# ACT writes the biases of keys and values into the banks ahead of the products, for 14 of 32 pairs

## The chip, the cores and the metric

One core of a Trainium2 chip. The time is the device time of one execution, in microseconds, as the median of several runs. A profiled execution gives a trace; its instants below are counted from the span's start. The names of the engines are PE (TensorE), DVE (VectorE), ACT (ScalarE), POOL (GpSimd) and SP (the queue that issues most DMAs).

## What is computed

One layer over 8 sequences of 1024 rows of width 256: attention with linear kernel features and no softmax, a residual and two layer norms, then a gated feed-forward of width 704 on weights and activations rounded in blocks of 16 to a four-bit grid, a residual and a layer norm. What the change touches is the first part:

```python
q = split(x @ Wq + bq);  k = split(x @ Wk + bk);  v = split(x @ Wv + bv)   # 16 heads of 16
q = elu(q) + 1;  k = elu(k) + 1
k = k / sqrt(sum(k * k, over a head) + eps)
attn = (q @ k.T) @ v          # per head; done as q @ (k.T @ v)
x = layernorm(x + layernorm_affine(x + attn @ Wo + bo))
# then w = four-bit blocks of the ffn weights, h = silu(x' @ wg) * (x' @ wu), x = layernorm(x + h' @ wd)
```

## The kernel before

The 8192 rows are 64 tiles of 128, worked in 32 pairs, four pairs to a sequence. Every engine has its own queue, written out by hand as a loop over steps p, and semaphores tie the queues together. Pairs 0 to 23 run alone (`first`); from step 24 (`MERGE`) on the second stage (`step`) is woven in, and from step 36 it runs alone.

PE in `first(p)`: transposes of x of pair p+1 (line 388), the products of keys and values of pair p (`kv_project`, lines 377 to 379 and the bias product at line 401), at some steps a turn of feed-forward weights (`weights_turn`, line 452), the accumulation of k.T v of pair p-2 (line 415), the query products of pair p-1, and at every fourth step `kv_out` (line 444). Every fp32 product is three fp32r products of high and low parts. The bias of the keys, and the 1 of elu + 1, are added by a small product of `rows` (ones times a two-row split of bk + 1) into the first 256 columns of a bank. Two pairs of banks take turns (`kv_banks`).

ACT: the high part of the transposes (line 574), the seeds of pair p-1 (lines 590, 591, 593), the queries of pair p-2 (599, 602), then the exponential of pair p's keys (608), the squares (613) and a weight chunk's conversion (581).

DVE: the low part of the transposes (756), query features (790), key features (800), then `v_bias` (806) that adds bv to the values while it takes them from the bank, sums of squares (813), the scales of a chunk of weights (760 to 768) and the rounding of a chunk (776, 778).

POOL: the Newton steps of pair p-1 (1036, 1038, 1040, 1043), normalised keys (1049, raises `k_hat`), x plus biases for the later residuals (1059, twice a pair), a weight chunk's scaling (1022), and the multiply that puts a rounded chunk back (1029, raises `w_deq`).

The feed-forward weights are rounded in 11 chunks during this stage, and their transposes (turns) are put at steps 8, 9, 12, 13, 16, 18, 22, 23, 24 and 25 (`WG_STEP`). A turn waits for the last chunk that it needs:

```python
def weights_turn(g):
    pe.wait_ge(w_deq, wg_chunks(g))
    after(pe, wT_lo, g)
```

The turns at steps 8, 12, 16, 18, 22 and 24 need 2, 4, 6, 7, 9 and 11 chunks. A chunk is put back in the pass of POOL just ahead of step 8, 12, 16, 18, 22 or 24.

Of the kernel before, what the change touches and what calls it, by code (L numbers as in the profile page):

```python
# [10 lines left out]
ALU = mybir.AluOpType  # L11
# [22 lines left out]
def build(nc, x, Wq, bq, Wk, bk, Wv, bv, Wo, bo, gamma, beta, w_gate, w_up, w_down, out):  # L34
# [21 lines left out]
    with ExitStack() as ctx:  # L56
# [3 lines left out]
        def sem(name):  # L60
            return ctx.enter_context(nc.semaphore(name))
# [14 lines left out]
        gamma_b = sb("gamma_b", [P, D])  # L76
        bq_c, bq_neg, bq_one = (sb(n, [P, KT]) for n in ("bq_c", "bq_neg", "bq_one"))
# [48 lines left out]
        bv_b, bo_b = words(9587, D), words(9843, D)  # L126
# [38 lines left out]
        def f32(a):  # L165
# [9 lines left out]
        wk_in, wv_in, wq_in, wffn_in, rows_in, bv_in, bq_in, xb_in, late_in = (  # L175
            sem(n) for n in ("wk_in", "wv_in", "wq_in", "wffn_in", "rows_in", "bv_in", "bq_in", "xb_in", "late_in"))
# [9 lines left out]
        xT_ps, xT_hi_s, xT_lo_s = sem("xT_ps"), sem("xT_hi_done"), sem("xT_lo_done")  # L186
        kv_ps, k_exp, k_feat, v_s, k_sq, k_ssq, k_se, k_log, k_seed = (
# [79 lines left out]

        def mo_bank(b):
            return Q_BANK if b < B - 1 else KV_BANK + 1
# [34 lines left out]
        def _(sp):  # L304
# [11 lines left out]
            sp.dma_start(beta_b[:, :], beta.partition_broadcast(P)).then_inc(xb_in, 16)  # L316
            load_x(2)
# [54 lines left out]
        def _(pe):  # L372
            def split_product(dst, stat, mov, n, ended=True, shared=False):

                for k in range(n):
                    (sh, sl), (mh, ml) = stat(k), mov(k)
                    nc.tensor.matmul(dst, sl, mh, start=(k == 0), stop=False, skip_group_check=shared)  # L377
                    nc.tensor.matmul(dst, sh, ml, start=False, stop=False, skip_group_check=shared)  # L378
                    last = nc.tensor.matmul(dst, sh, mh, start=False, stop=(ended and k == n - 1), skip_group_check=shared)  # L379
                return last  # L380
# [11 lines left out]
            def kv_project(p):  # L392
                pe.wait_ge(xT_lo_s, p + 1)
                after(pe, k_feat, kv_read(p))
                after(pe, v_s, kv_read(p))
                for jj in range(2):
                    bank = kv_banks(p) + jj
                    c = slice((p % PPB) * 2 * P + jj * P, (p % PPB) * 2 * P + (jj + 1) * P)
                    split_product(ps[:, bank, :], lambda k: (xT_hi[:, k, c], xT_lo[:, k, c]),
                                  lambda k: (wkv_hi[:, k, :], wkv_lo[:, k, :]), KT, ended=False, shared=True)  # L400
                    last = nc.tensor.matmul(ps[:, bank, 0:D], rows[:, D:], rows[:, 0:D], start=False, stop=True,  # L401
                                            skip_group_check=True)
                last.then_inc(kv_ps, 1)
# [161 lines left out]
        def _(act):  # L565
# [43 lines left out]

            def k_squares(p):  # L610
                act.wait_ge(k_feat, p + 1)
                after(act, k_ssq, p)
                nc.scalar.activation(ksq, kf[:, p % 2, :], ACT.Square).then_inc(k_sq, 1)
# [6 lines left out]
            def first(p):  # L620
# [16 lines left out]
                if p >= 7 and (p - 7) % PPB == 0 and (p - 7) // PPB < B:  # L637
                    kv_out_copy((p - 7) // PPB)
                if pair(p - 1):
                    k_seeds(p - 1)  # L640
# [98 lines left out]
        def _(dve):  # L739
# [63 lines left out]
            def v_bias(p):  # L803
                after(dve, kv_acc, p - 2)
                b = kv_banks(p)
                nc.vector.tensor_tensor(vb[:, p % 3, :, :], ps[:, b:b + 2, D:2 * D],
                                        bv_b[:, :].unsqueeze(1).broadcast_to([P, 2, D]), ALU.add).then_inc(v_s, 1)
# [366 lines left out]
```

## Time and profile before

| what | value |
|---|---|
| median of 3 runs | 708.73 us (708.36 to 708.86) |
| profiled execution, its own time | 708.65 us |
| its span, first to last instruction | 706.9 us |
| mean granted PE clock | 0.994 |
| PE busy | 687.4 us (97%) |
| PE weight loads busy | 603.9 us (85%) |
| POOL busy | 611.9 us (87%) |
| DVE busy | 593.9 us (84%) |
| ACT busy | 485.0 us (69%) |

How to read it: a busy PE is not PE at its peak, since matmuls are pipelined and their ends are modelled; the distance from one start to the next is what a product costs. An idle time stands in brackets with its releaser, which is the semaphore event that came last by the trace. A wait for several semaphores can name the wrong one.

### The profile page before, as it was taken

The page shows a single profiled execution, that of the slowest core. Times are in us where ns is not written, and L with a number is a line of the kernel's source. Part 1 is how long each engine was busy: PE and PEld are TensorE (multiplying, and loading weights), DVE is VectorE, ACT ScalarE, POOL GpSimd, SP SyncE. Part 2 cuts the span into 40 slices and gives each one's busy share as a digit, 9 for nine tenths or more (in the row PEclk, how much of TensorE's full clock was granted, in tenths as well). Part 3 has the DMA queues.
Part 4 walks back from the last instruction along what each step waited for, and adds up shares of the span by engine and source line. Part 5 has one row for each costly group of instructions (what it writes and reads, how often), then busy time and mean ns, then how long its engine had stood idle before and what let it go on. Part 6 is the DMA issues. An engine that isn't in the chain of part 4 may idle for free.

```text
span 706.9 us, 14230 instructions
## 1 busy us (share of the span) xinstructions
PE 687.4 (97%) x4370; PEld 603.9 (85%) x4370; DVE 593.9 (84%) x1448; ACT 485.0 (69%) x943; POOL 611.9 (87%) x951
## 2 busy tenths in 40 slices
PE   7999999999988999999999999999999999999995
PEld 6887878778866799999999999999999999999995
DVE  5788888885878888898898898998998898998774
ACT  4666766766667767767767767767767767767664
POOL 2989888987998999988988988988988988989766
PEclk9999999999999999999999999999999999999999
DMA  9443343344322021111111111111111111100001
GB/s 280 170 136 134 128 135 123 113 165 152 118 91 90 30 62 45 61 46 46 56 65 46 60 46 46 53 68 46 61 46 46 52 69 46 60 17 16 16 32 45
DMA packets 22272, 55.05 MB, mean 78 GB/s; under 512 B 2547, under 2 KB 5557, under 8 KB 22197
## 3 DMA queue, kind: packets, MB, share of 16 engines
q1 hardware_dynamic: 21776, 54.01, 22.5%
q8 instruction: 35, 0.57, 0.4%
q14 instruction: 41, 0.33, 0.2%
q10 hardware_dynamic: 420, 0.13, 0.1%
HBM read 28.90 MB, written 25.17 MB: 76 GB/s over the span
## 4 chain that ended last, share of the span: by engine, by line
PE 89%; POOL 4%; issue 3%; DVE 2%; ACT 1%; DMA 1%; SPq 0%; POOLq 0%; DVEq 0%; ACTq 0%
PE banks L377 23%; PE banks L379 22%; PE banks L378 22%; PE banks L519 8%; PE banks L490 7%; PE banks L415 2%; PE banks L388 2%; PE banks L533 1%; PE banks L532 1%; PE banks L401 1%; PE banks L444 1%; DMA arena<-in_L_attn_x_dram 1%; POOL arena L1126 1%; PE banks L452 1%; POOL lnbuf L1111 0%
## 5 line engine op out<-in xcount | busy, mean ns | idle before, releaser
L377 PE MATMUL banks<-wgu_hi,actT_lo 128*128 128x512 f32 (+1 forms) x384 | 149.8, 390 | 1.6 <-DVE resid L790 1.3
L378 PE MATMUL banks<-wgu_lo,actT_hi 128*128 128x512 f32 (+1 forms) x384 | 144.0, 375 | 0.0
L379 PE MATMUL banks<-wgu_hi,actT_hi 128*128 128x512 f32 (+1 forms) x384 | 143.3, 373 | 0.0
L1126 POOL TENSOR_TENSOR arena<-arena 128x960 f32<-128x960 f16 (+2 forms) x68 | 115.1, 1693 | 0.0
L688 ACT ACTIVATE arena<-banks 128x512 f32<-128x512 f32 x64 | 38.4, 599 | 111.7 <-PE banks L379 111.5
L1102 POOL TENSOR_TENSOR arena<-arena 128x704 f32<-128x704 f32 x64 | 89.1, 1392 | 21.1 <-DVE arena L907 19.0
L377 PE MATMUL banks<-wd_hi,actT_lo 128*128 128x256 f32 x320 | 100.1, 313 | 0.0
L920 DVE TENSOR_TENSOR actT_lo<-banks,actT_hi 128x512 fp32r<-128x512 f32 (+1 forms) x132 | 85.6, 674 | 16.9 <-ACT actT_hi L674 16.2
L379 PE MATMUL banks<-wd_hi,actT_hi 128*128 128x256 f32 x320 | 90.3, 282 | 0.0
L378 PE MATMUL banks<-wd_lo,actT_hi 128*128 128x256 f32 x320 | 90.2, 282 | 0.0
L377 PEld LDWEIGHTS banks<-wgu_hi,actT_lo 128*128 128x128 f32 x384 | 72.5, 189 | 11.2 <-DVE resid L790 1.7
L379 PEld LDWEIGHTS banks<-wgu_hi,actT_hi 128*128 128x128 f32 x384 | 72.2, 188 | 10.5
L378 PEld LDWEIGHTS banks<-wgu_lo,actT_hi 128*128 128x128 f32 x384 | 72.6, 189 | 7.6
L674 ACT ACTIVATE actT_hi<-banks 128x384 fp32r<-128x384 f32 (+2 forms) x132 | 63.3, 530 | 17.4 <-PE banks L519 17.4
L519 PEld LDWEIGHTS banks<-ident,arena 128*128 128x128 f32 x512 | 59.7, 140 | 12.5 <-DVE actT_lo L920 2.3
L660 ACT ACTIVATE arena<-arena 128x960 f16<-128x960 bf16 (+2 forms) x68 | 66.3, 975 | 5.8 <-POOL arena L1105 5.4
L519 PE MATMUL banks<-ident,arena 128*128 128x128 f32 x512 | 67.0, 272 | 3.4 <-DVE lnbuf L943 1.5
L929 DVE TENSOR_TENSOR arena<-arena,banks 128x512 f32<-128x512 f32 x64 | 43.9, 686 | 30.9 <-issue 26.4
L1111 POOL TENSOR_TENSOR lnbuf<-lnbuf,gamma_b 128x256 f32<-128x256 f32 x64 | 46.9, 732 | 24.4 <-ACT lnbuf L695 24.4
L1059 POOL TENSOR_TENSOR xs<-arena 128x512 f32<-128x512 f32 x48 | 61.6, 1304 | 6.6 <-DMA arena<-in_L_attn_beta_dram 6.6
L1089 POOL TENSOR_TENSOR rstd<-ve,mhalf 128x3 f32<-128x3 f32 x78 | 67.0, 858 | 0.0
L667 ACT ACTIVATE arena<-arena 128x960 uint16<-128x960 uint16 (+2 forms) x68 | 65.2, 958 | 2.2
(126 smaller groups left out, 1932.8 us busy)
## 6 DMA issues: line engine op xcount, KB each, us to landing
xs<-x_plus_scratch SPq DMA_DIRECT2D x32, 512.0 KB, 3.3
x_plus_scratch<-xs SPq DMA_DIRECT2D x24, 512.0 KB, 2.9
arena<-in_L_attn_x_dram SPq DMA_DIRECT2D x32, 256.0 KB, 3.6
out_dram<-arena SPq DMA_DIRECT2D x32, 256.0 KB, 2.1
x_plus_scratch<-arena SPq DMA_DIRECT2D x8, 512.0 KB, 2.9
resid<-in_L_ffn_w_down_dram SPq DMA_DIRECT2D x1, 704.0 KB, 7.7
resid<-in_L_ffn_w_gate_dram SPq DMA_DIRECT2D x1, 640.0 KB, 8.1
resid<-in_L_ffn_w_up_dram SPq DMA_DIRECT2D x1, 640.0 KB, 9.5
```

Of the source, the lines that this page charges most:

```text
L377: nc.tensor.matmul(dst, sl, mh, start=(k == 0), stop=False, skip_group_check=shared)
L378: nc.tensor.matmul(dst, sh, ml, start=False, stop=False, skip_group_check=shared)
L379: last = nc.tensor.matmul(dst, sh, mh, start=False, stop=(ended and k == n - 1), skip_group_check=shared)
L519: last = nc.tensor.transpose(ps[:, T_BANK + c // 4, (c % 4) * P:(c % 4 + 1) * P], va[:, (n + 1) % 2, c * P:(c + 1) * P], ident[:, :])
L660: nc.scalar.activation(vqb[n % 2][:, a // RW:b // RW, 0:RW].bitcast(F16), lines(halves(vy[:, n % 2, a:b])), ACT.Copy, scale=F16_ONE).then_ ...
L667: nc.scalar.activation(q, q, ACT.Copy, bias=ROUND_HALF).then_inc(half_s, 1)
L674: last = nc.scalar.activation(vT_hi[:, n % 2, a:whole, :], view[:, 0:whole - a, :], ACT.Copy)
L920: last = nc.vector.tensor_tensor(vT_lo[:, n % 2, a:b, :], view, f32(vT_hi[:, n % 2, a:b, :]), ALU.subtract)
L1059: nc.gpsimd.tensor_tensor(to[:, :, kind, :], xin[:, 2 * r:2 * r + 2, :], row[:, :].unsqueeze(1).broadcast_to([P, 2, D]), ALU.add).then_inc ...
L1089: nc.gpsimd.tensor_tensor(rstd[:, s, :], ve[:, :], mhalf[:, :].broadcast_to([P, 3]), ALU.pow).then_inc(pow_s, 1)
L1102: last = nc.gpsimd.tensor_tensor(blocks(vy[:, s, D:VW]), blocks(h[:, s, :]), each(inv[:, s, D // BLK:VB]), ALU.mult)
L1126: nc.gpsimd.tensor_tensor(blocks(va[:, (n + 1) % 2, a:b]), blocks(vqc[n % 2].bitcast(F16)[:, a:b]), each(s14[:, n % 2, a // BLK:b // BLK]) ...
```

## The change

For the 14 pairs from 2 to 23 that have no turn of weights in their step (`filled(p)`), ACT writes bk + 1 and bv into the pair's two banks in one activation of 128x1024 before the products, which then accumulate onto them and begin no new group. The two bias products of such a pair go, and DVE copies the values out of the bank where it added bv before. The key bias is loaded a second time, onto all partitions, and ACT adds 1.0 to it once. The activation for pair p+1 stands in ACT's `first(p)` ahead of the seeds of pair p-1. `bo_b` moves to a tile of its own.

```diff
+        bo_b = sb("bo_b", [P, D])
-        bv_b, bo_b = words(9587, D), words(9843, D)
+        bkv = words(9587, 2 * D)
+        bv_b = bkv[:, D:2 * D]
+        def filled(p):
+            return 2 <= p < MERGE and p not in WG_STEP
+        def fills(p):
+            return sum(filled(i) for i in range(p + 1))
@@ block.sync
             sp.dma_start(beta_b[:, :], beta.partition_broadcast(P)).then_inc(xb_in, 16)
+            sp.dma_start(bkv[:, 0:D], bk.partition_broadcast(P)).then_inc(bk_in, 16)
             load_x(2)
@@ kv_project
+                if filled(p):
+                    pe.wait_ge(kv_bias, fills(p))
                 for jj in range(2):
-                    split_product(ps[:, bank, :], lambda k: (xT_hi[:, k, c], xT_lo[:, k, c]),
-                                  lambda k: (wkv_hi[:, k, :], wkv_lo[:, k, :]), KT, ended=False, shared=True)
-                    last = nc.tensor.matmul(ps[:, bank, 0:D], rows[:, D:], rows[:, 0:D], start=False, stop=True,
-                                            skip_group_check=True)
+                    last = split_product(ps[:, bank, :], lambda k: (xT_hi[:, k, c], xT_lo[:, k, c]),
+                                         lambda k: (wkv_hi[:, k, :], wkv_lo[:, k, :]), KT, begun=filled(p), ended=filled(p),
+                                         shared=True)
+                    if not filled(p):
+                        last = nc.tensor.matmul(ps[:, bank, 0:D], rows[:, D:], rows[:, 0:D], start=False, stop=True,
+                                                skip_group_check=True)
@@ block.scalar
+            def kv_biases(p):
+                if p == 2:
+                    act.wait_ge(bk_in, 16)
+                    act.wait_ge(bv_in, 16)
+                    nc.scalar.activation(bkv[:, 0:D], bkv[:, 0:D], ACT.Copy, bias=1.0).then_inc(bk_one, 1)
+                    act.wait_ge(bk_one, 1)
+                act.wait_ge(k_feat, p - 1)
+                act.wait_ge(v_s, p - 1)
+                b = kv_banks(p)
+                nc.scalar.activation(ps[:, b:b + 2, :], bkv[:, :].unsqueeze(1).broadcast_to([P, 2, 2 * D]),
+                                     ACT.Copy).then_inc(kv_bias, 1)
@@ first(p), behind x_high(p + 1) and kv_out_copy
+                if filled(p + 1):
+                    kv_biases(p + 1)
                 if pair(p - 1):
                     k_seeds(p - 1)
@@ v_bias
-                nc.vector.tensor_tensor(vb[:, p % 3, :, :], ps[:, b:b + 2, D:2 * D],
-                                        bv_b[:, :].unsqueeze(1).broadcast_to([P, 2, D]), ALU.add).then_inc(v_s, 1)
+                if filled(p):
+                    nc.vector.tensor_copy(vb[:, p % 3, :, :], ps[:, b:b + 2, D:2 * D]).then_inc(v_s, 1)
+                else:
+                    nc.vector.tensor_tensor(vb[:, p % 3, :, :], ps[:, b:b + 2, D:2 * D],
+                                            bv_b[:, :].unsqueeze(1).broadcast_to([P, 2, D]), ALU.add).then_inc(v_s, 1)
```

## Rows read from the trace of the kernel before

**Rows 1.** Page, busy tenths in 40 equal slices of the span.

```profile
PE   7999999999988999999999999999999999999995
POOL 2989888987998999988988988988988988989766
```

**Rows 2.** Timeline of POOL, line 1036: start, duration (us), engine, line, operation, [idle before].

```profile
17.01 0.25 POOL L1036 TENSOR_TENSOR arena<-arena 128x32 f32<-128x32 f32 x1 [4.75 <-ACT arena L593]
...
49.40 0.25 POOL L1036 TENSOR_TENSOR arena<-arena 128x32 f32<-128x32 f32 x1 [0.71 <-ACT arena L593]
...
74.02 0.25 POOL L1036 TENSOR_TENSOR arena<-arena 128x32 f32<-128x32 f32 x1 [1.57 <-ACT arena L593]
...
123.17 0.25 POOL L1036 TENSOR_TENSOR arena<-arena 128x32 f32<-128x32 f32 x1 [1.23 <-ACT arena L593]
...
161.03 0.26 POOL L1036 TENSOR_TENSOR arena<-arena 128x32 f32<-128x32 f32 x1 [1.74 <-ACT arena L593]
```

**Rows 3.** Timeline of POOL, line 1029, chunks 2, 4, 7, 8 and 9.

```profile
55.28 0.84 POOL L1029 TENSOR_TENSOR resid<-arena,lnbuf 128x384 f32<-128x384 f16 x1 [0.20 <-DVE arena L778]
...
79.91 0.84 POOL L1029 TENSOR_TENSOR resid<-arena,lnbuf 128x384 f32<-128x384 f16 x1 [0.20 <-DVE arena L778]
...
116.29 0.84 POOL L1029 TENSOR_TENSOR resid<-arena,lnbuf 128x384 f32<-128x384 f16 x1 [0.20 <-DVE arena L778]
...
129.35 0.84 POOL L1029 TENSOR_TENSOR resid<-arena,lnbuf 128x384 f32<-128x384 f16 x1 [0.49 <-DVE arena L778]
...
141.47 0.83 POOL L1029 TENSOR_TENSOR resid<-arena,lnbuf 128x384 f32<-128x384 f16 x1
```

**Rows 4.** Timeline of PE, line 452, the turns at steps 8, 12, 18, 22.

```profile
56.27 0.63 PE L452 MATMUL banks<-ident,resid 128*128 128x128 f32 x4
...
80.85 0.63 PE L452 MATMUL banks<-ident,resid 128*128 128x128 f32 x4
...
117.34 0.60 PE L452 MATMUL banks<-ident,resid 128*128 128x128 f32 x4
...
142.40 0.63 PE L452 MATMUL banks<-ident,resid 128*128 128x128 f32 x4 [1.03 <-DVE actT_lo L756]
```

**Rows 5.** Timeline of DVE, two roundings (line 778) and line 756.

```profile
129.01 0.26 DVE L778 TENSOR_SCALAR arena<-arena 128x384 uint16<-128x384 uint16 x1
...
139.57 1.24 DVE L778 TENSOR_SCALAR arena<-arena 128x384 uint16<-128x384 uint16 x1
140.73 0.68 DVE L756 TENSOR_TENSOR actT_lo<-banks,actT_hi 128x512 fp32r<-128x512 f32 x1
```

**Rows 6.** Timeline of PE, a bias product of step 3 and its successor.

```profile
25.45 0.28 PE L401 MATMUL banks<-rows 128*128 128x256 f32 x1
25.57 0.39 PE L377 MATMUL banks<-wkv_hi,actT_lo 128*128 128x512 f32 x1
```

**Rows 7.** Groups of ACT by form: shape, xcount, busy us, mean ns, idle before.

```profile
L585 ACT ACTIVATE wd_hi<-banks 128x512 fp32r<-128x512 f32 x2 | 1.2, 590 | 0.0
L585 ACT ACTIVATE wd_hi<-banks 128x256 fp32r<-128x256 f32 x2 | 0.8, 376 | 0.0
```

**Rows 8.** Timeline of ACT, steps 1 (seeds of pair 0) and 3 (exponential).

```profile
16.28 0.32 ACT L590 ACTIVATE arena<-arena,eps_k 128x32 f32<-128x32 f32 x1 [0.27 <-DVE arena L813]
16.51 0.30 ACT L591 ACTIVATE arena<-arena,eps_k 128x32 f32<-128x32 f32 x1
...
27.27 0.69 ACT L608 ACTIVATE arena<-banks,mone 128x512 f32<-128x512 f32 x1 [0.62 <-PE banks L401]
```

**Rows 9.** Two PE stops, and windows (PEclk third from the end).

```profile
203.28 0.77 PE L377 MATMUL banks<-wkv_hi,actT_lo 128*128 128x512 f32 x1 [2.57 <-DVE arena L806]
...
238.03 1.09 PE L519 MATMUL banks<-ident,arena 128*128 128x128 f32 x8 [1.51 <-DVE lnbuf L943]
...
204.00:205.00 1.00, 1.00 (x4) 0.81 (x3) 1.00 (x2) 1.00 (x4) 0.77 (x2) 0.50 0.06 16
...
230.00:240.00 10.00, 8.49 (x45) 7.05 (x44) 8.28 (x24) 7.16 (x14) 9.53 (x14) 1.00 0.15 52
```

## What I expect of it

> **What bounds the kernel now.** I read the page's slices first: TensorE is at nine tenths in nearly every slice, GpSimd at eight or nine through the first third [rows 1]. The change lies wholly in that third, the stage of keys, values and queries, where TensorE's timeline is gapless for most pairs. So the tempting sum is "TensorE work removed = time gained". Then I asked who else could not go faster, and followed GpSimd through the same stage. From 17 us on it is gapless too, save where it waits for ACT's seeds before line 1036, the first operation of a pair's Newton step. There are seven such waits up to 161 us; five stand in [rows 2], the others are at 98.60 and 110.40. Between two of them its own work sets the pace. And TensorE depends on it: `weights_turn` waits for `w_deq`, which GpSimd's line 1029 raises. I put the end of each such multiply beside the start of the turn that needs it [rows 3, 4]: 56.12 against 56.27 (pair 8), 80.75 against 80.85 (pair 12), 117.13 against 117.34 (pair 18), 142.30 against 142.40 (pair 22); pair 16's looks like pair 12's. At the last of them TensorE did wait, 1.03 us. The row names DVE's line 756, but that ended at 141.41 [rows 5]; GpSimd had just finished. So at five places TensorE and GpSimd arrive nearly together, and TensorE alone can't gain across them.
>
> **What is removed.** 28 bias products, two in each of 14 pairs (2 to 7, 10, 11, 14, 15, 17, 19 to 21). One lasts 0.28 us, but the next product starts 0.12 after it [rows 6], and that distance is the price: 0.23 us a pair, 3.2 us in all. DVE's addition of the value bias becomes a copy of the same 128x512 from the same banks. No row shows one; I take it at no gain and no loss, since it reads and writes as many elements. At best it saves 0.1 us a pair on an engine that isn't the late one at the turns; at worst see rival 4.
>
> **What is added.** ACT writes 128x1024 into the banks, 14 times. No row has that shape: 128x256 took 0.376 and 128x512 0.590 us [rows 7], 0.21 per 256 columns, so 1024 come to about 1.02 us, an estimate. An instruction on ACT starts some 0.1 before the one ahead of it ends (16.28 + 0.32 against 16.51) [rows 8], so it holds the queue for 0.93. Bounds: 0.6 (no dearer than one 512) and 1.3 (as two of them). Does ACT have the time? It waits 0.62 for the products of a pair in the third line of [rows 8] and again for transposes, so part of the copy fills waits. Counted from start to start, a pair keeps ACT for 4.4 us, waits for DVE's features in it; 5.3 with the copy, against 5.41 that a pair then takes on TensorE. With a weight chunk's 0.5 it falls behind for one pair and catches up at the next without a copy. TensorE's new wait on the written banks doesn't bite: the copy for pair p+1 is issued a whole pair ahead, some 3 us early. The copy's own waits (features and values of pair p-1) are met before it is reached, since ACT's squares of that pair stand ahead of it.
>
> But behind the copy stand the seeds, and on them GpSimd's whole queue. Of the seven waits, two belong to an ACT pass that holds a copy: pair 0's (idle 4.75) and pair 18's (idle 1.23) [rows 2]. At the first there is also the one-time addition of 1.0 to the key bias, 128x256, 0.38. ACT had 0.27 idle there [rows 8]. So the first seeds come 0.93 + 0.38 - 0.27, 1.0 us, late.
>
> The load of the key bias (128 KB) stands behind beta's and ahead of two x loads on SP's queue. GpSimd's first bias work waits for beta, which is ahead, so it isn't moved. The x loads may come 0.5 us later; TensorE's transposes of pair 2 follow the product before them directly, so there is some slack. Zero, at most 0.5.
>
> **The sum, place by place** (shift against before, minus is earlier).
> - Up to turn 8: GpSimd starts at +1.0; its wait at pair 6 gives back 0.71; TensorE had 0.15 in hand and needs some 0.08. Turn 8 comes at +0.25, instead of the -1.4 of TensorE's own saving. ACT's lag around pair 4 may add 0.2. I take +0.4.
> - Pair 10: -0.23, so +0.17 at its seeds, and GpSimd's 1.57 idle there covers its own lag. Turn 12: TensorE would be at -0.06, the chunk comes at about +0.15.
> - Pairs 14 and 15: the first counts, the second is lost in turn 16's tie: -0.1. Pair 17: turn 18 at -0.25.
> - Pair 18's seeds: -0.25 + 0.93 = +0.7. GpSimd's queue alone would allow less. At 129.35 GpSimd had waited 0.49 for DVE [rows 3], which this lag uses up: +0.2.
> - Turn 22 needs the chunk that follows: +0.2. The 0.69 us saved in pairs 19 to 21 only lengthen TensorE's wait there.
> - Behind it no pair is changed. Pair 24's seeds come at 161.03 after 1.74 idle, so GpSimd follows TensorE there, and all that comes later keeps the shift.
>
> That is +0.2 us on the profiled execution's own 708.65 (span 706.9 and 1.75 around it), 708.85; the median of the runs is 708.73, within 0.1. I forecast **708.9 us**. Of TensorE's 3.2 us, 1.4 go into waiting at turn 8 and 0.7 at turn 22; the rest is balanced by what the copy holds back. With the copy's bounds (it counts about once at turn 8 and once at pair 18) and 0.3 for GpSimd's small waits on DVE, this case spans 708.0 to 709.8.
>
> **Rivals.**
> 1. TensorE's clock falls in the longer wait: slower. At turn 22 TensorE would stand still for 1.03 + 0.2 + 0.25 + 0.69 = 2.2 us. Before, it stood 2.57 us ahead of 203.28 and the granted clock was then 0.50, that is 1.2 GHz: in that state a product took 0.77 instead of 0.50, and the next seven were slower too, some 1.5 us lost. A stop of 1.51 left the clock at 1.00 [rows 9]. 2.2 lies between, nearer to the one that fell. TensorE leads from turn 22 to pair 24's seeds, so the loss would reach the end: 710.4. It decides from some length between 1.5 and 2.57 us on. Chance 0.18.
> 2. The ties don't bind, because chunks are ready earlier once TensorE and DVE run ahead. Then the savings reach the end: 707.1 if half of them do, 705.5 if all. For it: only one of the five turns shows a wait. Against it: GpSimd's queue is full from 17 to 49 us, and nothing of it is removed. Chance 0.14.
> 3. The copy is dear. At 1.6 us it holds 0.67 more at both places: 710.2, and ACT is the last at each filled pair. Decides from about 1.5 us on. Chance 0.04.
> 4. DVE's new copy is held by GpSimd, as the rounding of a chunk is: the same line took 0.26 in one place and 1.24 in another, where it ended only with GpSimd's multiply [rows 5]. If each copy lost 0.6 on average, the sums, seeds and chunks behind it would come that much later at turn 8 and pair 18: 709.9. Against it: the rounding works within SBUF tiles, the copy reads a bank, as the addition did that never was long. Chance 0.04.
>
> The Trainium skill (SBUF — State Buffer, Who interferes with whom) says that a copy can take the port pair that VectorE and GpSimd share, and that one of them then blocks wholly; by that rule rival 4 would be the forecast. The Trainium skill (VectorE: DVE Perf Modes, Why PSUM operands drop a tier) says that a PSUM operand rules that mode out; by this one rival 4 can't happen. No row of before shows a copy from a bank.
>
> **Chances.** Forecast's case 0.60, rivals 0.18, 0.14, 0.04, 0.04. About 0.2%, 1.4 us, is what a measurement of this kernel can tell from no change: 707.3 to 710.1. Faster: rival 2, 0.14. Slower: most of rivals 1, 3 and 4, 0.23. Same: the rest, 0.63. The range, 706.9 to 710.4, leaves out the fuller half of rival 2 and the outer half of rivals 1 and 3.
>
> **What would show it.** Right: from pair 3 to 5 TensorE's transposes 5.41 us apart; a wait of some 1.6 us at turn 8 and 2.2 at turn 22, whatever engine the row names; GpSimd's first Newton step at 18.0 instead of 17.0 us, and no idle at pair 6; turn 22 at 142.4 to 142.8. Wrong: turn 8 near 55 us (GpSimd wasn't the tie), a copy of over 1.3 us, DVE's copy over 0.9, a granted clock under 1 behind turn 22, or TensorE waiting for `kv_bias`.

## The result, and the profile after

The changed kernel takes 712.22 us (median of 6 runs, 710.94 to 715.35), the kernel before in the same session 708.62 (6 runs, 707.27 to 708.92): ratio 1.0061, interval 1.0041 to 1.0081. It is slower by 0.6%, some 3.6 us, where 0.2 us were forecast. (Two more executions on record took 712.61 and 714.75 us; the ratio includes them.) The profiled execution is the longest, 715.35 us (span 713.6, mean clock 0.987); the others lie at 0.989 to 0.993. Its shifts add up to some 3 us more than the median's, so its instants show where time goes and not how much of it goes in a typical execution.

All line numbers moved: 377 to 379 are now 389 to 391, 401 is 417, 415 is 431, 444 is 460, 452 is 468 (TensorE); 574 is 590, 590 to 593 are 606 to 609 (ACT); 756 is 787, 776 and 778 are 807 and 809, 790 is 821, 829 is 863 (DVE); 1029 and 1036 are 1063 and 1070 (GpSimd). New are 631 and 636 on ACT and 838 on DVE. In the kernels of the experiments they move again by a few lines.

First what the new instructions cost, from the groups of ACT and DVE by form (count, busy us, mean ns, idle before):

```profile
L636 ACT ACTIVATE banks<-arena 128x1024 f32<-128x1024 f32 x14 | 14.4, 1026 | 0.0
L631 ACT ACTIVATE arena<-arena 128x256 f32<-128x256 f32 x1 | 0.4, 408 | 0.0
L840 DVE TENSOR_TENSOR arena<-banks,arena 128x512 f32<-128x512 f32 x18 | 12.3, 684 | 0.0
L838 DVE COPY arena<-banks 128x512 f32<-128x512 f32 x14 | 9.6, 683 | 0.0
```

The write into the banks is 1.03 us, and a copy on DVE takes just what the addition took. Behind them, the first seeds and GpSimd's first Newton step, against 17.01 with 4.75 idle [rows 2]:

```profile
15.86 0.41 ACT L631 ACTIVATE arena<-arena 128x256 f32<-128x256 f32 x1
16.30 1.03 ACT L636 ACTIVATE banks<-arena 128x1024 f32<-128x1024 f32 x1
17.27 0.31 ACT L606 ACTIVATE arena<-arena,eps_k 128x32 f32<-128x32 f32 x1
...
17.98 0.25 POOL L1070 TENSOR_TENSOR arena<-arena 128x32 f32<-128x32 f32 x1 [5.39 <-ACT arena L609]
```

So far as forecast. The surprise is the timeline of TensorE in step 6: it stops for 2.17 us before the accumulation of pair 4, and its `kv_out` afterwards takes 1.91 us. The last row is the turn of step 8.

```profile
42.51 0.39 PE L391 MATMUL banks<-wkv_hi,actT_hi 128*128 128x512 f32 x1
45.06 0.69 PE L431 MATMUL banks<-arena 128*64 128x64 f32 x16 [2.17 <-DVE arena L863]
...
46.80 0.63 PE L390 MATMUL banks<-actT_lo,wq_hi 128*128 128x512 f32 x1
47.22 0.63 PE L391 MATMUL banks<-actT_hi,wq_hi 128*128 128x512 f32 x1
47.65 1.91 PE L460 MATMUL banks<-wo_sb,arena 128*128 128x256 f32 x4
...
58.88 0.63 PE L468 MATMUL banks<-ident,resid 128*128 128x128 f32 x4 [0.18 <-POOL resid L1063]
```

The same stretch of the kernel before, which the prediction didn't look at, on TensorE's timeline:

```profile
43.87 0.28 PE L401 MATMUL banks<-rows 128*128 128x256 f32 x1
44.10 0.68 PE L415 MATMUL banks<-arena 128*64 128x64 f32 x16
...
46.20 1.02 PE L444 MATMUL banks<-wo_sb,arena 128*128 128x256 f32 x4
```

And on its DVE:

```profile
42.17 0.78 DVE L778 TENSOR_SCALAR arena<-arena 128x384 uint16<-128x384 uint16 x1
42.88 0.68 DVE L756 TENSOR_TENSOR actT_lo<-banks,actT_hi 128x512 fp32r<-128x512 f32 x1
43.48 0.47 DVE L829 TENSOR_TENSOR arena<-banks,headmask 128x128 f32<-128x128 f32 x2
```

DVE's `mask_heads` empties the bank in which the first sequence was summed, at 43.48 + 0.47 = 43.95, and TensorE begins the next sum in that bank at 44.10: a sixth tie (a place where an engine begins just when another engine has finished what it needs), with 0.15 us in hand and no wait in the row. In the changed kernel the mask starts at 44.45, 0.97 later, by as much as the first seeds are late, while TensorE is there 1.2 us earlier (45.06 - 2.17 = 42.89 against 44.10), by ten bias products of 0.12. 0.97 + 1.2 is the wait. That nothing has to be taken off for the 0.15 shows that they were no slack: here, where TensorE plainly waits, it also starts only 0.14 behind the mask's end (44.92 against 45.06), and 0.11 behind GpSimd's multiply at turn 22. DVE of the changed kernel:

```profile
41.95 1.16 DVE L807 TENSOR_SCALAR arena<-arena 128x384 uint16<-128x384 uint16 x1
43.15 0.78 DVE L809 TENSOR_SCALAR arena<-arena 128x384 uint16<-128x384 uint16 x1
43.85 0.68 DVE L787 TENSOR_TENSOR actT_lo<-banks,actT_hi 128x512 fp32r<-128x512 f32 x1
44.45 0.47 DVE L863 TENSOR_TENSOR arena<-banks,headmask 128x128 f32<-128x128 f32 x2
```

The second place is turn 22, where 1.03 us of idle [rows 4] became 2.94. The last product before it, the turn and the next turn on TensorE of the changed kernel:

```profile
142.82 0.28 PE L417 MATMUL banks<-rows 128*128 128x256 f32 x1
146.04 1.09 PE L468 MATMUL banks<-ident,resid 128*128 128x128 f32 x4 [2.94 <-issue]
147.06 1.12 PE L431 MATMUL banks<-arena 128*64 128x64 f32 x16
...
155.94 0.60 PE L468 MATMUL banks<-ident,resid 128*128 128x128 f32 x4
```

The multiply on GpSimd that this turn needs:

```profile
145.10 0.83 POOL L1063 TENSOR_TENSOR resid<-arena,lnbuf 128x384 f32<-128x384 f16 x1
```

And the granted clock, in windows of the changed kernel (length, then busy us of PE, PE load, DVE, ACT, POOL, then PEclk, DMA share, GB/s):

```profile
40.00:50.00 10.00, 7.83 (x44) 6.03 (x43) 8.51 (x17) 5.43 (x11) 9.12 (x12) 0.83 0.36 119
140.00:150.00 10.00, 7.06 (x40) 5.47 (x40) 8.11 (x14) 5.14 (x12) 9.42 (x15) 0.78 0.43 140
147.00:151.00 4.00, 4.00 (x24) 3.25 (x24) 3.06 (x4) 1.53 (x3) 3.72 (x5) 0.50 0.16 46
```

GpSimd's multiply ends at 145.93 and the turn starts at 146.04. From this turn to the next it takes 9.90 us, and 6.99 in the kernel before (142.40 to 149.39): 2.9 us, over which the granted clock is 0.50 from 146 to 152 us.

The whole ledger of this execution, as shift against before: first Newton step +1.0; accumulation of step 6 +1.0 (45.06 against 44.10); turn 8 +2.6 (58.88 against 56.27), so 1.6 us more behind the first stop, where the clock is 0.50 from 47 to 50 us; turns 12, 16 and 18 +2.6, +2.55, +2.45; pair 18's seeds +3.4 (126.60 against 123.17); turn 22 +3.6; the turn of step 23 and pair 24's seeds (167.58 against 161.03) +6.55; end of the span +6.7.

### The profile page after: what moved, and what is told of

Read it like the earlier page. It is cut to its first block, busy times and chain, and to the rows that moved or that the text cites. A ratio compares the mean times of both kernels' runs of the same rounds, so it can differ in the third digit from the quotient of the medians.

```text
span 713.6 us, 14218 instructions
## 1 busy us (share of the span) xinstructions
PE 689.3 (97%) x4342; PEld 603.3 (85%) x4342; DVE 596.9 (84%) x1448; ACT 496.0 (69%) x958; POOL 612.8 (86%) x951
## 4 chain that ended last, share of the span: by engine, by line
PE 80%; DVE 5%; POOL 5%; issue 5%; ACT 4%; DMA 1%; SPq 0%; POOLq 0%; DVEq 0%; ACTq 0%
PE banks L389 20%; PE banks L391 19%; PE banks L390 19%; PE banks L535 8%; PE banks L506 7%; PE banks L431 1%; PE banks L400 1%; DVE arena L831 1%; PE banks L460 1%; PE banks L549 1%; PE banks L548 1%; ACT banks L636 1%; ACT arena L642 1%; DMA arena<-in_L_attn_x_dram 1%; POOL arena L1160 1%
## 5 line engine op out<-in xcount | busy, mean ns | idle before, releaser
L506 PE MATMUL banks<-mo,resid 128*128 128x256 f32 x256 | 65.6, 379 | 0.0
## 6 DMA issues: line engine op xcount, KB each, us to landing
resid<-in_L_ffn_w_down_dram SPq DMA_DIRECT2D x1, 704.0 KB, 8.9
```

The source lines that it names most:

```text
L506: last = nc.tensor.matmul(ps[:, at_bank(u), 0:D], resid[:, u, m * P:(m + 1) * P], mo[:, u // TPB, m, :], start=(m == 0), stop=(m == KT - 1))
```

## The experiments

Two theories ran against each other. **A**: the 3.2 us of left-out products are real but TensorE's work is tied to DVE and GpSimd at turns and at the mask, the copies on ACT make those two late, and the stops that result lower the clock. **B**: the copies cost something of their own at every step. Ratios are to the kernel before, run between the others on the same chip; its medians were 708.3 to 709.3.

Apart from medians I use one distance, free of what differs in the first 13 us of each execution (ACT's first exponential of keys starts between 11.6 and 14.9 us, whatever the kernel): from that exponential to a milestone. Each such distance is read from one profiled execution, and its scatter from execution to execution isn't known. The diffs are shortened.

**Bias products left out, nothing in their place** (the keys of 14 pairs lack their bias and the 1 of elu + 1).

```diff
-                    split_product(..., KT, ended=False, shared=True)
-                    last = nc.tensor.matmul(ps[:, bank, 0:D], rows[:, D:], rows[:, 0:D], start=False, stop=True, ...)
+                    last = split_product(..., KT, ended=filled(p), shared=True)
+                    if not filled(p):
+                        last = nc.tensor.matmul(...)
```

> The kernel before with the 28 bias products of the 14 pairs left out and nothing in their place (those keys lack their bias); ACT, DVE and the DMAs are as before. Theory A (TensorE is tied to what DVE and GpSimd finish, and a wait of over 2 us lowers its clock): the 3.2 us do not reach the end. TensorE waits at step 6 for the masked heads and at turns 8 and 22 for a chunk; turn 22 stays within 0.5 us of 142.4, and the time is 707.5 to 709 without a fall of the clock, up to 710.5 with one. Theory B (ACT's copy is what costs): without the copy the saving arrives, turn 22 at 139.5 or so, 705.5 us.

Measured: 708.35 us, ratio 0.9995 (0.9977 to 1.0012), as A had it. 3.2 us less work on TensorE shows no gain, though the interval leaves room for 1.6 us. The profiled execution, 705.8 us and the second fastest of ten, does show a part. Turn 22 stands at 139.52, the instant that B named, but this execution began early. Counted from the first exponential (11.86, against 13.37 before) step 6 comes 0.8 us earlier than in the kernel before, turn 18 1.6, turn 22 1.4 and the end 1.3. So some 1.3 of the 3.2 us arrive there. DVE and GpSimd come earlier too when TensorE feeds them earlier, but not by as much. The stops stand where the ties are:

```profile
41.80 0.69 PE L422 MATMUL banks<-arena 128*64 128x64 f32 x16 [0.38 <-DVE arena L836]
...
139.52 0.63 PE L459 MATMUL banks<-ident,resid 128*128 128x128 f32 x4 [2.00 <-issue]
```

**Copies kept, bias products kept too** (the products start their group anew, DVE adds bv as before).

```diff
-                    last = split_product(..., KT, begun=filled(p), ended=filled(p), shared=True)
-                    if not filled(p):
-                        last = nc.tensor.matmul(...)
+                    last = split_product(..., KT, ended=False, shared=True)
+                    last = nc.tensor.matmul(...)
```

> The changed kernel with ACT's writes into the banks and TensorE's wait on them kept, but the products begin anew and keep their bias products, and DVE adds the value bias as before: only the cost of the copy. Theory A: TensorE arrives later at every tie, so the copy shows only where the seeds were the last: GpSimd's first step at 18.0, pair 18's seeds 0.9 later; 709 to 710 us, no fall of the clock up to 200 us. Theory B: ACT is the late one by itself, 712 us, with TensorE waiting for the features or banks.

Measured: 712.2 us, ratio 1.0061 (1.0038 to 1.0084), the changed kernel's. This is B's time; A had given 709 to 710. With the run above it is a square: no gain from leaving the products out shows without copies, and none with copies. The copies cost 3.6 us, whether or not TensorE's work is less. Counted from the first exponential, the profiled execution is 1.0 us behind that of before in step 6 (the late first seeds, seen there as a wait of 0.94), another 0.9 by turn 18 (waits of 0.31, 0.31 and 0.24 at transposes behind copies), another 1.15 at turn 22 (a stop of 2.17, against 1.03), and 3.1 at the end. Its clock stayed at 1.00 up to 200 us, as A had it, so these 3.1 us are the copies' without any part of a slow clock.

**The mask ahead of the rounding of a chunk** (changed kernel).

```diff
-                if p >= 6 and (p - 6) % PPB == 0 and (p - 6) // PPB < B - 1:
-                    mask_heads((p - 6) // PPB)
@@ end of DVE's first(p), behind k_sums
+                if p >= 5 and (p - 5) % PPB == 0 and (p - 5) // PPB < B - 1:
+                    mask_heads((p - 5) // PPB)
```

> The changed kernel, but DVE masks the heads at the end of steps 5, 9, ... ahead of the rounding of a chunk, instead of behind it at steps 6, 10, ... . Theory A: the wait of 2.17 us at 45 us goes, with it the fall of the clock there; turn 8 comes at 56.7 to 57.2 instead of 58.9 after a wait of about 1.5, and the end is 1.5 to 2 us earlier than the changed kernel in a run with the same falls later on: 709.5 to 711. Theory B: the wait moves elsewhere, 712.

Measured: 710.37 us, ratio 1.0037 (1.0019 to 1.0056), as A had it: by the medians half the loss, though this interval and the changed kernel's overlap. The profile is clearer. The stop of step 6 is gone, the clock of 40 to 50 us is 1.00, and turn 8 comes 42.94 us behind the first exponential (14.32), against 42.90 in the kernel before and 45.55 in the changed one. The stop of turn 22 and its slow clock remain, the next turn coming 9.83 us later:

```profile
43.86 0.69 PE L431 MATMUL banks<-arena 128*64 128x64 f32 x16
...
144.00 1.09 PE L468 MATMUL banks<-ident,resid 128*128 128x128 f32 x4 [2.69 <-issue]
```

**Seeds ahead of the copy** (changed kernel).

```diff
-                if filled(p + 1):
-                    kv_biases(p + 1)
                 if pair(p - 1):
                     k_seeds(p - 1)
+                if filled(p + 1):
+                    kv_biases(p + 1)
```

> The changed kernel with ACT's writes into the banks moved from ahead of the seeds to right behind them. Theory A (the writes cost where seeds, turns and GpSimd's queue wait for them; 1.0 us at the first seeds and 0.9 at pair 18's, and 0.3 at each of steps 9, 13 and 18 by way of the keys' exponential and the weights' high part): the first two go, the 0.3s stay. GpSimd's first step comes 3.6 us after the first exponential instead of 4.65, pair 18's seeds some 1.5 to 2 us earlier than in the changed kernel; 709.5 to 711 us, less where the wait at turn 22 stays without a fall of the clock. Theory B (ACT is short of time as such): the same sum of work, so 712 as before this edit.

Measured: 714.33 us, ratio 1.0065 (1.0038 to 1.0093), not better. Three of the seven executions lie at 710.1 to 711.4 us, about where A had them, and four at 714.3 to 714.8, above both theories. In the profiled one, of the slower four, the first Newton step is on time (3.64 us behind the first exponential, as in the kernel before), but the stop of step 6 is longer. Both its stops are followed by a slow clock:

```profile
46.28 0.69 PE L431 MATMUL banks<-arena 128*64 128x64 f32 x16 [2.71 <-DVE arena L863]
...
146.33 0.90 PE L468 MATMUL banks<-ident,resid 128*128 128x128 f32 x4 [2.15 <-DVE actT_lo L787]
```

ACT shows what holds it. TensorE starts its transposes 5.4 us apart in this stretch, and ACT its `x_high` (line 590) 5.65 to 6.05 apart from 20.7 to 38.1 us. In each round it waits 0.84 us for DVE's features, and mostly 0.27 for DVE's sums, while DVE waits for ACT's query exponential (2.38, 1.35, 2.31, 1.39 and 0.93 us before line 821, from 24 to 47 us). With a copy in each of steps 1 to 6 the delay doesn't go away when the copy is put elsewhere in the round; it only moves from the seeds to the queries.

**Query products ahead of the turn and the accumulation, in steps 1 to 23**, in the changed kernel and in the kernel before.

```diff
+                if pair(p - 1):
+                    q_project(p - 1)
                 if p in WG_STEP:
                     pe.wait_ge(xT_lo_s, p + 2)
                     weights_turn(WG_STEP[p])
                 if pair(p - 2):
                     kv_accumulate(p - 2)
-                if pair(p - 1):
-                    q_project(p - 1)
```

> The changed kernel with TensorE's query products of pair p-1 ahead of the turn of weights and of the accumulation of pair p-2 in steps 1 to 23: 1.5 us of products stand where it waited. Theory A: the waits at 45 and 143 us shrink by 1.5 to under 1.5 us, no fall of the clock before 200 us, time 708.5 to 710, because the ties still hold. Theory B: no change against the changed kernel, 712.

> The kernel before with the query products ahead of the turn of weights and of the accumulation in steps 1 to 23, nothing else. Theory A: before has only one wait, of 1.0 us at turn 22, to fill; behind every turn the transposes wait 0.5 to 0.8 for the weights' low part: 708 to 710 us, no gain. So what the same edit gave the changed kernel (some 4 us) is its waits and the fall of the clock. Theory C (the order of the products is better by itself): 704.5 us.

Measured: 708.0 us, ratio 1.0000 (0.9991 to 1.0010) for the changed kernel, 709.36 us, 1.0023 (1.0012 to 1.0034) for the kernel before. The first is below what A gave (708.5 to 710), the second as A had it. So the same reordering wins 4 us on the one and loses 1.6 on the other. TensorE now has 1.4 us of other work where it stopped; its stop at turn 22 is 1.52 and the clock stays:

```profile
142.63 0.63 PE L468 MATMUL banks<-ident,resid 128*128 128x128 f32 x4 [1.52 <-issue]
```

**Seeds first, and query products first in steps 6, 8, 10, 14, 18 and 22 alone.**

> The changed kernel with the seeds ahead of ACT's writes, and with the query products first only in steps 6, 8, 10, 14, 18 and 22, where TensorE waited for the masked heads or a chunk. Theory A: waits under 1.5 us, no fall of the clock before 200 us, the ties of GpSimd as without the writes: turn 22 at 127.5 to 128.5 us after the first exponential, 706 to 707.5 us, 0.2 to 0.3% under before. Theory B: 708 or more.

Measured: 708.77 us, ratio 1.0009 (0.9995 to 1.0023). A's 706 to 707.5 was missed, and B's 708 or more met. Seeds first again adds nothing. In the profiled execution stops of 1.35 and 1.00 us stood in step 6 close together (before 46.74 and 48.43), and the granted clock behind them was 0.50 from 48 to 51 us.

**Turns of weights one step later, no bias products** (14 pairs' keys lack their bias, as in the first run).

```diff
-            ready = CHUNK_STEP[(max(cols) + P - 1) // CW] + 4
+            ready = CHUNK_STEP[(max(cols) + P - 1) // CW] + 5
```

> The kernel before without the bias products of the 14 pairs (as in the run without biases), and every turn of weights one step later, so that its chunk is long there. Theory A (TensorE is tied to GpSimd at the turns): with the ties gone the waits at the turns go, and more of the 3.2 us arrives than the 1.3 of the profile without later turns: 704.5 to 706.5 us, until GpSimd's own queue holds TensorE at the accumulations. Theory D (something else holds TensorE): the same 708.3 median and the waits reappear at other lines.

Measured: 704.0 us, ratio 0.9952 (0.9936 to 0.9968), as A had it or a little better. The first clear gain: moving the turns away from the chunks that they need frees what left-out products alone couldn't.

**The same move in the changed kernel, in the kernel before, and with a second tie loosened.** Edits: the line above, with the same 14 pairs named one by one; for the third also the mask's; for the fourth the query products first in steps 6, 10, 14, 18 and 22.

> The changed kernel with each turn of weights one step later, over the same 14 pairs. Theory A (the 3.2 us of bias products are lost because turns of weights and the accumulation of step 6 are tied to VectorE and GpSimd; the copies cost 1.0 us at the first seeds and little else): the stops at the turns go, that in step 6 stays (2.2 us, with its fall of the clock), so 704.0 + 1.0 + 1 to 3 = 706.0 to 708.0 us, ratio 0.997 to 0.9995. Rival (the copies on ScalarE cost something in every step wherever the turns are): 28 bias products are given back and 14 copies cost 0.3 to 0.6 us each, 709 to 712 us, ratio 1.001 or more.

> The kernel before with each turn of weights one step later and nothing else. Theory A: turn 22 waits 1.0 us for GpSimd in the kernel before, which goes, and nothing else moves: 707.2 to 708.2 us, ratio 0.998 to 1.000, so that the kernel without the bias products (704.0 with turns later) is 3.2 to 4 us ahead of it, which is the price of the 28 products. Rival (the moved turns are what gave the 4.3 us): 704 to 705 us, ratio 0.994 to 0.995.

> The changed kernel with turns of weights one step later and the masking of a batch's sums ahead of the rounding. Theory A: both ties are loosened, what is left is the 1.0 us at the first seeds and 0.2 to 0.3 us at each of three transposes: 704.0 + 1.0 + 0.9 = 705 to 706.5 us, ratio 0.995 to 0.9975, faster than the run with turns later alone by 0.5 to 2 us. Rival (masking early only moves VectorE's delay to the next step): equal to the run with turns later alone within 0.5 us.

> The changed kernel with turns of weights one step later, and with the query products ahead of the accumulation in steps 6, 10, 14, 18 and 22 alone. Theory A: TensorE has some 2.8 us of other work where it waited in step 6, so the wait of 2.2 us and the fall of the clock go: 705 to 706.5 us. Rival (the query exponentials come earlier on ScalarE and push the transposes' rounding back): 707 us or more.

Measured: 710.01 us, ratio 1.0021 (1.0010 to 1.0031); 707.61, 0.9991 (0.9981 to 1.0001); 706.75, 0.9984 (0.9973 to 0.9994); 706.61, 0.9984 (0.9976 to 0.9993). The first is a miss, 2 us above what A gave, and B's time. The second is as A had it: the moved turns by themselves give nothing that can be told. The other two are just outside A's times (to 706.5). The profiled execution of the first is the fastest of its twelve, 707.78 us, and no clock fell in it before 200 us. Its waits are 1.64 in step 6, 0.35, 0.35, 0.49, 1.11, and 0.85 at the accumulation of step 22. Three of them (0.35, 0.35, 1.11) stand at transposes whose bank is held up by a weight's low part, which a copy delayed on ACT. The run with no bias products and turns later has 0.40 in step 6, 0.16 in place of the 1.11, and 0.90 at step 22 without any copy, so not all of these waits are the copies'. The distance to the turn of step 23 (table below) puts the 14 copies at 135.98 - 132.36 = 3.62 us, more than the 3.2 that the products give: B has a part of the truth. Two of the waits as they stand with turns later and the mask early, on TensorE:

```profile
64.06 0.65 PE L400 MATMUL banks<-ident,arena 128*128 128x128 f32 x4 [0.35 <-DVE wd_lo L813]
...
126.11 0.66 PE L400 MATMUL banks<-ident,arena 128*128 128x128 f32 x4 [1.11 <-DVE wgu_lo L813]
```

**Which copies cost?** Pair 2 left as it was (turns in place); then copies for pairs 3, 4, 5, 6, 7, 11, 15 and 21 alone, with turns in place, and with turns later and the mask early.

```diff
-            return 2 <= p < MERGE and p not in WG_STEP
+            return p in (3, 4, 5, 6, 7, 11, 15, 21)
```

> The changed kernel in which pair 2 is left as it was (its bias product stays, no copy for it), so 13 copies and 26 products. Theory A: the 1.0 us at the first seeds and as much of the wait of step 6 were the cost of that one copy; the wait of step 6 falls from 2.2 to about 1.2 us and the clock stays: 1.0 + 0.8 us less than the changed kernel, 709.8 to 711.2 us, ratio 1.002 to 1.004. Rival (ScalarE is full in steps 2 to 6, at 5.3 us a step with a copy in each, and would be late without the first one too): the wait of step 6 stays near 2 us, with a fall of the clock: 711.5 to 712.5 us.

> The changed kernel with the copies for pairs 3, 4, 5, 6, 7, 11, 15 and 21 alone, whose 16 bias products are worth 1.9 us, and the turns where they were. Left out are those copies with which a wait was found: pair 2 (first seeds), 10 and 14 (transposes of steps 9 and 13), 17, 19, 20 (before the turn of step 22). Theory A: the turn of step 22 waits for the chain behind pair 18's seeds as in the kernel before, with 1 to 2 us in place of 2.9, and the products left out are lost in it: 708.0 to 709.5 us, ratio 0.9995 to 1.0015. Rival (any copy costs as much as a bias product pair saves, wherever it stands): half of the loss stays, 710 to 711 us.

> The same eight copies, with the turns one step later and the masking ahead of the rounding. Theory A: the run with fourteen copies had waits of 0.36, 0.35, 0.35, 0.49 and 1.11 us behind copies and 1.0 at the first seeds, 3.3 us with the last one in; without them and with 12 bias products more (1.4 us) it is 1.5 to 2 us ahead of that run: 704.5 to 705.5 us, ratio 0.9945 to 0.996. Rival (what counts is only the number of bias products left out, the waits close up elsewhere): 708 us, ratio 0.999 or more.

Measured: 711.52 us, ratio 1.0039 (1.0025 to 1.0053); 708.74, 1.0004 (0.9995 to 1.0012); 705.67, 0.9962 (0.9949 to 0.9976). Without pair 2's copy the wait of step 6 is 1.28 us, as A had it, and that run's profile (708.97 us, its fastest execution) shows no slow clock before 200 us, yet six of its seven other executions have a mean clock of 0.991 to 0.994. The median is 0.7 us under the changed kernel's, where A had 1.8; against the kernel before, the ratios differ by 1.6 us, with intervals that overlap, so how much that one copy costs isn't shown. Without all six copies that had a wait behind them the loss is gone, but the 1.9 us of products left out don't show either, as A had it. With the ties loosened it is 0.2 us above what A gave and far from the rival's 708. No idle time is noted on TensorE between 20 and 160 us, and this version is 0.4% faster than the kernel before and 1.0% faster than the changed one.

**The moves alone, and the moves with no bias products** (as in the first run).

> The kernel before with both moves (turns one step later, masking ahead of the rounding) and no copy. It is the control for the run with eight copies and both moves (ratio 0.9962). Theory A: with the ties loosened the 16 bias products are worth their 1.9 us, so this kernel is at 0.9985 to 0.9995, 707.2 to 708.0 us, 2 us behind that run. Rival (the moves alone made that run fast, the copies nothing): 705.7 us, ratio 0.996.

> Both moves, and the 28 bias products of the 14 pairs left out with nothing in their place (the keys of these pairs then lack their bias and the 1). Against the run with both moves alone (ratio 0.9975; its turn of step 23 starts 134.15 us after the first keys' exponential). Theory A (with the ties loosened each bias product is worth its 0.12 us): that distance becomes 134.15 - 3.2 = 130.95 us, and the median 702 to 703.5 us. Rival (VectorE, ScalarE or GpSimd bound part of the stage even then): the distance stays above 132 us.

Measured: 705.77 us, ratio 0.9975 (0.9962 to 0.9987), and 704.07, 0.9927 (0.9911 to 0.9943). The first hits its rival's time: by the medians (705.77 and 705.67) the eight copies add nothing to the moves, by the ratios 0.9 us, with intervals that overlap. The second is above A's median, and its distance is as A had it. The seven executions of the first lie in two groups, 705.6 to 705.8 and 707.7 to 708.3, and the profiled one is of the slower group, so I also compare by the distance to the turn of step 23. It starts here, with both moves alone, with no bias products, and with eight copies (x3 where the view's window ends inside the turn of four transposes):

```profile
148.53 0.60 PE L452 MATMUL banks<-ident,resid 128*128 128x128 f32 x4
```

```profile
145.70 0.49 PE L459 MATMUL banks<-ident,resid 128*128 128x128 f32 x3
```

```profile
145.71 0.49 PE L468 MATMUL banks<-ident,resid 128*128 128x128 f32 x3
```

| kernel, turns later | first exponential | turn of step 23 | distance | ratio |
|---|---|---|---|---|
| before | 13.02 | 147.56 | 134.54 | 0.9991 |
| before, mask early | 14.38 | 148.53 | 134.15 | 0.9975 |
| no bias products | 13.26 | 145.62 | 132.36 | 0.9952 |
| no bias products, mask early | 14.85 | 145.70 | 130.85 | 0.9927 |
| 14 copies | 11.96 | 147.94 | 135.98 | 1.0021 |
| 14 copies, mask early | 13.34 | 146.91 | 133.57 | 0.9984 |
| 8 copies, mask early | 13.20 | 145.71 | 132.51 | 0.9962 |

In these single executions, with both ties loosened, 28 bias products are worth 134.15 - 130.85 = 3.30 us, against 3.2 estimated from one distance between starts. 14 copies cost 133.57 - 130.85 = 2.72, and leave 0.6 of it. Eight well placed ones leave 134.15 - 132.51 = 1.64 of the 1.85 that their 16 products are worth. Of these three the medians bear out only the first (the ratios differ by 3.4 us); by the ratios the 14 copies with both moves are 0.6 us slower than the moves alone, and not 0.6 faster, within intervals that overlap.

## Why the prediction was wrong

**What held.** The price of a bias product (0.12, shown by the last table), the write's 1.02 us (1.03), the first seeds 1.0 us late (17.98 against 17.01), DVE's copy at no gain and no loss. The last settles rival 4: 0.683 us on average over 14 copies, 0.684 for the addition. The Trainium skill (VectorE: DVE Perf Modes, Why PSUM operands drop a tier) had excluded the faster mode, and with it the blocking, for a PSUM operand; the trace agrees. TensorE never waited for `kv_bias`, and its transposes came 5.40 us apart from pair 3 on. Rival 3 is out by the 1.03 us. (Rival 4's 0.6 us at two places would have made 710.1 and not 709.9; nothing hangs on it.) Rival 2, savings that arrive because ties don't bind, is out in full: with the products left out alone the time was 708.35. Its half isn't quite (0.9977, the edge of that interval, is 1.6 us), and some 1.3 of the 3.2 us arrived in that run's profiled execution. With the mask early, turn 8 came 0.04 us and turn 22 0.65 us late against before, counted from the first exponential; the sum had +0.25 to +0.4 and +0.2. So up to turn 22 it was close, once the tie that it lacked was out of the way.

**The step that failed first: the list of ties.** The prediction counted five, all of them turns that need a chunk, because I followed one engine, GpSimd. The tie with DVE's mask in step 6, 0.15 us of slack in the kernel before, wasn't looked for. So the term "Up to turn 8", +0.4 behind a wait of 1.6, was wrong: the wait came two steps earlier, was 2.17 long because both sides moved (DVE +0.97, TensorE -1.2), and the granted clock fell behind it, which made +2.6 at turn 8, where only 0.18 of idle was left. Moving the mask alone took the +2.6 at turn 8 away and gave back 1.85 of 3.6 us of the medians.

**The second: where copies cost.** The sum counts the copy at two places, the seeds of pair 0 and of pair 18, for which GpSimd waits. That left out what else stands behind ACT's copy: the keys' exponential, the weights' high part, and behind that DVE's low part, for which TensorE's transposes wait (0.28 at 67.88 and 92.44 in the changed kernel, none there before). The estimate of ACT's time was right (5.26 us a round with a copy, transposes 5.40 apart), but it leaves 0.14 a round to catch up with, and a round with a chunk's conversion took 5.67. So "catches up at the next without a copy" was too kind: the 1.0 of the first seeds was still there in step 6, as the mask's 0.97, and seeds first only moved the delay, to 2.71 us in step 6. The copies alone, with every bias product kept and no slow clock before 200 us, cost 3.1 us in that run's profiled execution.

**The third: rival 1's size.** It was the right mechanism at turn 22, with a chance of 0.18 and +1.5 us. The wait was 2.94 instead of 2.2 and the slow clock behind it cost 2.9, not 1.5, since the clock stayed at 0.50 for longer. From turn 22 to the next turn the changed kernel took 2.9 us more than the kernel before, and the run with the mask early 2.8, both at 0.50 for some 6 us; the run with the seeds first took 1.5 more (8.48), at 0.50 for some 3 us. The price of 1.5 was read from a place with 3 us of it. Why it lasts longer in some executions isn't shown. And nothing in the sum allowed for a stop of more than 2 us elsewhere.

**What stays open.** How long a stop the clock bears. In profiled executions it stayed at 1.00 after stops of 1.52, 2.00, 2.17 and 2.68 us, the last in the run without pair 2's copy:

```profile
142.70 0.63 PE L468 MATMUL banks<-ident,resid 128*128 128x128 f32 x4 [2.68 <-issue]
```

It also stayed after 1.64 in step 6 of the run with turns later. It fell after others of 2.15, 2.17, 2.69, 2.71 and 2.94, and after 1.35 and 1.00 close together. So the length of a stop doesn't decide it by itself. A place that every one of these kernels has shows the same. Near 200 us TensorE stops for 2.51 to 2.64 us, in the kernel before ahead of 203.28 [rows 9], the row from which the prediction took its price. In ten of the nineteen profiled executions the clock fell behind this stop. In the other nine it held, and fell behind a stop of 2.50 to 2.56 us some 12 us later, which in the first ten is only 0.9 to 1.2 long. Here the changed kernel with turns later, at clock 1.00 from 203 to 206 us and 0.50 from 215 on:

```profile
202.27 0.47 PE L389 MATMUL banks<-wkv_hi,actT_lo 128*128 128x512 f32 x1 [2.59 <-DVE arena L840]
...
214.39 0.74 PE L431 MATMUL banks<-arena 128*64 128x64 f32 x16 [2.56 <-POOL arena L1083]
```

Such differences between executions may be a part of why the times of one kernel spread over 1 to 5 us; that isn't shown. So the split of the changed kernel's 3.6 us into stops and slow clock isn't settled for the median, only for the profiled execution. The load of the key bias wasn't tried by itself: in the window from 8 to 10 us the DMAs moved 149 GB/s against 344 in the kernel before (114 to 149 in all twelve kernels with the load, 221 to 360 in the seven without), but ACT's first exponential started at 13.33 against 13.37, so no cost of it shows.

## What to carry to other kernels

Where one engine's queue is gapless, look for ties, not for waits: for each of its semaphore waits, set the end of the work waited for beside the start of the work behind the wait. 0.10 to 0.15 us between them was no slack here: TensorE started as late behind the other engine's end where it plainly waited. Work removed from such an engine becomes in part a stop at the first tie, and a stop of over some 2 us can cost as much again by the clock (2.94 and then 2.9 at turn 22; in other executions nothing). So move the tied steps first (one line here, of no effect that could be told by itself on the kernel before, and some 3 us once the products were gone), and only then take work out. When work is moved onto a second engine, count all that stands behind it in that queue, through to who waits for each.

## What the runs showed of the hardware

ACT's write of 128x1024 fp32 from SBUF into PSUM took 1.03 us, on the line through the 0.376 and 0.590 us of activations of 256 and 512 columns [rows 7]. DVE's copy of 128x512 fp32 out of PSUM took 0.683 us, no less than an addition of the same shape with a second operand. At 1.2 GHz (PEclk 0.50) a product of 512 columns showed 0.63 instead of 0.39 us, and starts came 0.43 instead of 0.23 apart. The same stop of 2.5 to 2.6 us near 200 us was followed by 1.2 GHz in ten profiled executions and not in nine.
